# Fifteen tiles of 256 rows and nine of 128 in place of 23 of 256, each operation of three tiles at a step of its own

## The reference

```python
logits = h @ router_weight.T + router_bias
top_vals, top_idx = jax.lax.top_k(logits, 2)
scores = zeros_like(logits).at[arange(T)[:, None], top_idx].set(softmax(top_vals))
gate_up = einsum('th,ehj->etj', h, gate_up_proj) + gate_up_proj_bias[:, None, :]
gate, up = minimum(gate_up[..., ::2], 7), clip(gate_up[..., 1::2], -7, 7)
act = (up + 1) * gate * sigmoid(gate * 1.702)
expert_out = einsum('eti,eih->eth', act, down_proj) + down_proj_bias[:, None, :]
out = x + einsum('te,eth->th', scores, expert_out)
```

## Time and profile before

| | us |
|---|---|
| median of 3 runs | 971.46 |
| lowest, highest | 971.12, 971.56 |
| the profiled execution's own time | 971.87 |
| its span, first to last instruction | 970.1 |
| of it up to the first matmul of an expert | 535.9 |
| of it the expert stage | 434.2 |

### The profile page before, as it was taken

One profiled execution on the slowest core, in us unless ns is written; L12 is line 12 of the kernel. 1 busy time (PEld: TensorE's weight loads), 2 busy tenths in 40 slices (PEclk: granted clock), 3 DMA queues, 4 the chain that ended last, 5 costly groups with the idle time before them and its releaser, 6 DMA issues.

```text
span 970.1 us, 17745 instructions
## 1 busy us (share of the span) xinstructions
PE 865.6 (89%) x7104; PEld 702.1 (72%) x7104; DVE 655.5 (68%) x1356; ACT 464.4 (48%) x735; POOL 314.5 (32%) x348
## 2 busy tenths in 40 slices
PE   5889799897998989889763799999999999999995
PEld 3556567574665756667432799999999999999993
DVE  5654646656466564655564589889888888888872
ACT  4433343333424333333420467677677676676652
POOL 2112221323213232032223233453453454544512
PEclk9999799998999989899675799999999999999998
DMA  8273134171431716126303477687687787786810
GB/s 318 80 251 116 42 131 138 56 253 46 161 104 67 242 57 205 49 73 231 148 11 107 173 239 209 238 242 216 237 234 219 238 235 219 249 220 201 263 55 0
DMA packets 49541, 159.47 MB, mean 164 GB/s; under 512 B 6164, under 2 KB 6420, under 8 KB 40243
## 3 DMA queue, kind: packets, MB, share of 16 engines
q0 software_dynamic: 22368, 98.52, 32.0%
q1 hardware_dynamic: 27090, 59.82, 18.1%
HBM read 103.04 MB, written 58.94 MB: 167 GB/s over the span
## 4 chain that ended last, share of the span: by engine, by line
PE 82%; DVE 6%; ACT 5%; issue 3%; POOL 1%; DMA 1%; SPq 0%; POOLq 0%; another core or an unknown queue 0%; ACTq 0%; DVEq 0%
PE quad L562 9%; PE quad L563 9%; PE quad L564 9%; PE bank L434 7%; PE bank L344 7%; PE bank L337 6%; PE bank L338 6%; PE bank L339 6%; PE bank L370 5%; PE bank L372 4%; PE bank L371 4%; PE quad L395 3%; ACT pt L999 3%; PE quad L415 2%; PE bank L472 2%
## 5 line engine op out<-in xcount | busy, mean ns | idle before, releaser
L562 PE MATMUL quad<-xh,eh 128*128 128x256 f32 x736 | 210.8, 286 | 5.1 <-issue 3.6
L564 PE MATMUL quad<-xh,el 128*128 128x256 f32 x736 | 209.7, 285 | 0.0
L563 PE MATMUL quad<-xl,eh 128*128 128x256 f32 x736 | 209.0, 284 | 0.0
L835 DVE TENSOR_TENSOR el<-raw,eh 128x2048 fp32r<-128x2048 f32 x69 | 158.6, 2299 | 8.8 <-ACT eh L1022 8.8
L562 PEld LDWEIGHTS quad<-xh,eh 128*128 128x128 f32 x736 | 141.0, 192 | 7.5 <-issue 3.8
L563 PEld LDWEIGHTS quad<-xl,eh 128*128 128x128 f32 x736 | 140.6, 191 | 1.8
L564 PEld LDWEIGHTS quad<-xh,el 128*128 128x128 f32 x736 | 139.8, 190 | 0.0
L1022 ACT ACTIVATE eh<-raw 128x2048 fp32r<-128x2048 f32 x69 | 131.6, 1909 | 0.0
L687 DVE TENSOR_REDUCE mx<-quad 128x8 f32<-128x2048 f32 x32 | 73.3, 2292 | 59.7 <-PE quad L395 58.3
L1080 ACT ACTIVATE up<-quad,gb 128x256 f32<-128x256 f32 x92 | 43.6, 474 | 109.8 <-DVE ga L908 109.0
L1196 POOL DMA_INDIRECT out<-ys,ti x46 | 82.1, 1785 | 32.5 <-ACT ys L1094 19.3
(11 more groups left out here) (192 smaller groups left out, 1852.2 us busy)
## 6 DMA issues: line engine op xcount, KB each, us to landing
hs<-wh SPq DMA_DIRECT2D x16, 2084.0 KB, 14.9
xt<-in_x SPq DMA_DIRECT2D x8, 512.0 KB, 5.2
cr<-in_ctxT SPq DMA_DIRECT2D x8, 512.0 KB, 3.9
xb<-in_x SPq DMA_DIRECT2D x8, 512.0 KB, 6.3
out<-xb SPq DMA_DIRECT2D x16, 256.0 KB, 2.0
pt<-in_w SPq DMA_DIRECT2D x3, 1024.0 KB, 6.7
raw<-in_wgb SPq DMA_DIRECT2D x1, 1028.0 KB, 8.1
pt<-in_w SPq DMA_DIRECT2D x4, 256.0 KB, 6.1
```

The costliest lines, as they stand in the source:

```text
L562: e.matmul(o, lh, xh[p][:, c, :], start=c == 0, stop=False)
L563: e.matmul(o, lh, xl[p][:, c, :], start=False, stop=False)
L564: done = e.matmul(o, ll, xh[p][:, c, :], start=False, stop=c == C - 1)
L835: e.tensor_tensor(wl[p][:, part, :], raw[part][:, 0:GW], wh[p][:, part, :].bitcast(F32), ALU.subtract).then_inc(S_(f"e_lo{part}"), 1)
```

## The change

**Two kinds of tile.** `KIND` is S B B seven times, then S B S: 15 large tiles (B, 256 rows) and 9 small ones (S, 128 rows), 24 in all. An expert with u blocks of 128 rows gets large tiles for pairs of blocks and a small one for an odd block; when pairs outnumber the large tiles the rest of them goes to small ones. `tiles()` decides this on DVE by 18 intervals of tiles instead of 8, with arrays of 24 x 18 where it had 23 x 8. One small tile always belongs to expert 0.

**Small tiles.** For these PE holds the rows (128 of them stationary) and moves the weights, 12 matmuls of 512 columns for gate and 12 for up, each half in a bank of its own, plus one matmul of 16 partitions that adds the bias, from a one-hot matrix `oh16` and a table `gbt` that the new `bias_table` makes in the attention stage. The result has rows on partitions. DVE bounds gate and up and multiplies them, ACT takes the sigmoid, each over 128 x 512. Then PE transposes it four times (`turn_act`), and ACT and DVE split it into `ah` and `al`. One `down`, one gather, one add. The three weight parts and their six splits are the same as for a large tile.

**Steps.** `EX` holds a step for each operation of a group of three tiles: S, the B behind it, and the B behind that, called C. The next group's are 92 later. Units, banks, rows and transposes are counted through both kinds.

**The rest.** In `AT` and `ONCE` some steps change; on the engines this moves the transposes of a batch's first k head on PE, and some constants of the first batch on DVE. `bias_table` adds four operations on DVE and two loads of 16 rows.

```diff
-NT = 23
+NT = 24
+BIG = 15
...
+KIND = "SBB" * 7 + "SBS"
...
+BI = before({"B": 1, "S": 0})
+SI = before({"B": 0, "S": 1})
+RI = before({"B": 2, "S": 1})
+UI = before({"B": 4, "S": 2})
...
+SLOT = ["SBC"[i % 3] if KIND[i] == "B" else "S" for i in range(NT)]
...
+GROUP = 92
+EX = {
+    "S": {
+        "turn": -29, "u0": 6, "u1": 8, "act": 35, "down0": 58, "V.xl": -31, "V.gate0": -2, "V.gate1": 18, "V.sl": 32,
...
+def step(i, name):
+    return EX[SLOT[i]][name] + GROUP * (i // 3) + (2 * GROUP // 3 if SLOT[i] == "S" and i % 3 else 0)
+TILES = defaultdict(list)
+for _i in range(NT):
+    for _n in EX[SLOT[_i]]:
+        TILES[step(_i, _n), _n].append(_i)
...
-    "x0": -25, "x1": -19, "k0": -14, "q0": -11, "k1": 4, "q1": 5, "v0": 29, "v1": 35, "hk0": 4, "hq0": 9, "hk1": 24,
+    "x0": -25, "x1": -19, "k0": -14, "q0": -11, "k1": 4, "q1": 5, "v0": 30, "v1": 35, "hk0": -2, "hq0": 9, "hk1": 24,
...
+            def gates_or_ups(i, h):
+                p = i % 2
+                o = bank_of_tile(i, h)
+                for c in range(C):
+                    off = (c % 2) * 1024 + h * 512
+                    rh = wh[p][:, c // 2, off:off + 512]
+                    rl = wl[p][:, c // 2, off:off + 512]
+                    e.matmul(o, xh[p][:, c, 0:128], rh, start=c == 0, stop=False)
+                    e.matmul(o, xh[p][:, c, 0:128], rl, start=False, stop=False)
+                    e.matmul(o, xl[p][:, c, 0:128], rh, start=False, stop=False)
+                P.wait_ge(S_("oh16"), SI[i] + 1)
+                P.wait_ge(S_("gbt"), 1)
+                e.matmul(o, oh16[SI[i] % 2][32:48, :], gbt[:, h * 512:(h + 1) * 512], start=False, stop=True).then_inc(S_("gate_up"), 1)
+            def turn_act(i):
+                P.wait_ge(S_("s_act"), SI[i] + 1)
+                turn(turn_bank(("s", i, 0)), sgs, 4).then_inc(S_("s_turned"), 1)
...
             def down(i, r):
                 p = i % 2
+                n = RI[i] + r
...
-                P.wait_ge(S_("act_lo"), C * i + C)
+                if KIND[i] == "B":
+                    P.wait_ge(S_("act_lo"), C * BI[i] + C)
+                else:
+                    P.wait_ge(S_("s_lo"), SI[i] + 1)
                 P.wait_ge(S_("e_lo2"), i + 1)
...
-            turn_x(0)
-            for i in range(NT + 1):
+                bank_done(P, 6 + n % 2)
+                P.wait_ge(S_("scaled"), n - 1)
+                three(bank[6 + n % 2], lh, ll, rh, rl).then_inc(S_("down"), 1)
+            for s in range(EFIRST, ELAST):
+                for i in tile_at(s, "turn"):
+                    turn_x(i)
+                for i in tile_at(s, "act"):
+                    turn_act(i)
                 for m in range(C):
-                    if i < NT:
-                        gate_up(i, m)
-                    if m == 0 and i + 1 < NT:
-                        turn_x(i + 1)
-                    if m >= 2 and i > 0:
-                        down(i - 1, m - 2)
+                    for i in tile_at(s, f"u{m}"):
+                        if KIND[i] == "B":
+                            gate_up(i, m)
+                        else:
+                            gates_or_ups(i, m)
+                for r in range(2):
+                    for i in tile_at(s, f"down{r}"):
+                        down(i, r)
...
+                P.wait_ge(S_("d_gb"), 32)
+                for h in range(2):
+                    own.done(e.tensor_copy(gbt[:, h * D:(h + 1) * D], gbr[h]))
+                own.wait()
+                for h in range(2):
+                    i = e.scalar_tensor_tensor(out=gbt[:, h * D:(h + 1) * D], in0=gbt[:, h * D:(h + 1) * D].bitcast(F32), scalar=NLG, in1=gbr[h],
+                                               op0=ALU.mult, op1=ALU.add)
...
+                own.done(e.memset(b18[:, :, 0:1], 1.0))
+                own.done(e.tensor_tensor(cn[:], run[:], EBASE, ALU.subtract))
...
+                chain(e.tensor_tensor(cn[:], cn[:], M0, ALU.max))
+                chain(e.tensor_tensor(ci[:], cn[:], CEIL, ALU.add))
+                own.done(e.tensor_scalar(cj[:], ci[:], 7, None, ALU.logical_shift_right))
+                chain(e.tensor_scalar(ck[:], ci[:], 8, None, ALU.logical_shift_right))
+                own.done(e.tensor_copy(uf[:], cj[:]))
+                chain(e.tensor_copy(af[:], ck[:]))
+                own.done(e.tensor_tensor_scan(an[:], onef[:, 0:NE], af[:], 0.0, ALU.mult, ALU.add))
+                chain(e.scalar_tensor_tensor(out=sf[:], in0=af[:], scalar=-2.0, in1=uf[:], op0=ALU.mult, op1=ALU.add))
+                own.done(e.tensor_scalar(ends[:, 1:9], an[:], 2.0, None, ALU.mult))
...
+                own.done(e.tensor_tensor(b18[:, :, 1:NS + 1], PI.unsqueeze(2).to_broadcast([128, NT, NS]),
+                                         ends[:].unsqueeze(1).to_broadcast([128, NT, NS]), ALU.is_ge))
...
+                own.done(e.scalar_tensor_tensor(out=vb[:, 10:18], in0=sf[:], scalar=-128.0, in1=LASTS, op0=ALU.mult, op1=ALU.add))
+                chain(e.tensor_tensor(ohG[:], b18[:, :, 0:NS], b18[:, :, 1:NS + 1], ALU.subtract))
+                for n, v in ((0, vb), (1, vend)):
+                    chain(e.tensor_tensor(pv[:], ohG[:], v[:].unsqueeze(1).to_broadcast([128, NT, NS]), ALU.mult))
                     chain(e.tensor_reduce(bv[:, n, :], pv[:], AX, ALU.add))
...
+                chain(e.tensor_tensor(ohE[:], ohG[:, :, 1:9], ohG[:, :, 10:18], ALU.add))
+                chain(e.tensor_tensor(ohE[:, :, 0], ohE[:, :, 0], ohG[:, :, 0], ALU.add))
+                chain(e.tensor_tensor(pv[:, :, 0:NE], ohE[:], cmt[:, 0:NE].unsqueeze(1).to_broadcast([128, NT, NE]), ALU.mult))
+                chain(e.tensor_reduce(Ei[:], pv[:, :, 0:NE], AX, ALU.add))
+                chain(e.tensor_scalar(gf[:, :, 0], Ei[:], 128.0, PIDX, ALU.mult, ALU.add))
+                e.tensor_copy(wx[:], gf[:, :, 0]).then_inc(S_("wx_set"), 1)
...
+            def gates(i):
+                u = UI[i]
+                P.wait_ge(S_("gate_up"), u + 1)
+                P.wait_ge(S_("s_act"), SI[i])
+                e.tensor_scalar(gus[:, 0, :], bank[u % 4], LIMIT, None, ALU.min).then_inc(S_("gate_in"), 1)
+            def ups(i):
+                u = UI[i] + 1
+                P.wait_ge(S_("gate_up"), u + 1)
+                e.tensor_scalar(gus[:, 1, :], bank[u % 4], LIMIT, -LIMIT, ALU.min, ALU.max).then_inc(S_("gate_in"), 1)
+                P.wait_ge(S_("gate_in"), u + 1)
+                chain(e.scalar_tensor_tensor(out=gus[:, 1, :], in0=gus[:, 1, :], scalar=1.0, in1=gus[:, 0, :], op0=ALU.add, op1=ALU.mult))
+                P.wait_ge(S_("s_sigm"), SI[i] + 1)
+                e.tensor_tensor(sgs[:], gus[:, 1, :], sgs[:], ALU.mult).then_inc(S_("s_act"), 1)
+            def turned_low(i):
+                p = i % 2
+                k = 4 + TURNS.index(("s", i, 0)) % 2
+                P.wait_ge(S_("s_hi"), SI[i] + 1)
+                e.tensor_tensor(al[p][:, :, 0:128], bank[k].rearrange("p (c n) -> p c n", c=4),
+                                ah[p][:, :, 0:128].bitcast(F32), ALU.subtract).then_inc(S_("s_lo"), 1)
...
-            fetch_x(0)
-            fetch_x(1)
-            fetch_w(1, 0)
-            fetch_w(1, 1)
-            for i in range(NT + 1):
-                for m in range(C):
-                    if i < NT:
-                        if m in (2, 3) and i + 2 < NT:
-                            fetch_w(i + 2, m - 2)
-                        if m == 3 and i + 1 < NT:
-                            fetch_w(i + 1, 2)
-                    if m == 0 and i + 2 < NT:
-                        fetch_x(i + 2)
-                    if m == 3 and i > 0:
-                        add_rows(i - 1)
+                        out, bass.IndirectOffsetOnAxis(ap=ti[:, 2 * i + r:2 * i + r + 1], axis=0), ys[n % 2][:], None,
+                        bounds_check=T - 1, oob_is_err=False, compute_op=ALU.add).then_inc(S_(f"d_add{n % 2}"), 16)
+            for s in range(EFIRST, ELAST):
+                for i in tile_at(s, "G.x"):
+                    fetch_x(i)
+                for part in range(3):
+                    for i in tile_at(s, f"G.w{part}"):
+                        if i > 0:
+                            fetch_w(i, part)
+                for i in tile_at(s, "G.add"):
+                    add_rows(i)
...
```

More of the change, by code:

```diff
@@ L37, with before, rows, drained @@
 DW = 2056
+KIND = "SBB" * 7 + "SBS"
+def before(size):
+    return [0] + [int(n) for n in np.cumsum([size[k] for k in KIND])]
+BI = before({"B": 1, "S": 0})
+SI = before({"B": 0, "S": 1})
+RI = before({"B": 2, "S": 1})
+UI = before({"B": 4, "S": 2})
+def rows(i):
+    return range(RI[i + 1] - RI[i])
+def drained(u):
+    i = next(i for i in range(NT) if u <= UI[i + 1])
+    return u, 4 * BI[i] + (u - UI[i] if KIND[i] == "B" else 0)
+SLOT = ["SBC"[i % 3] if KIND[i] == "B" else "S" for i in range(NT)]
@@ new lines, with tile_at @@
+GROUP = 92
+EX = {
[4 rows of a table added]
+    },
[7 rows of a table added]
+    },
[6 rows of a table added]
+        "G.add": 116,
+    },
+}
+def step(i, name):
```

(50 more changed lines are left out.)

304 lines of the change are left out of this document (175 added, 129 removed), and 29 rows, old and new, of tables (AT, EX).

## The result

The changed kernel takes 937.38 us (median of 4 runs, 931.86 to 938.46), the kernel before 971.29 beside it: 0.9647 of before, 95% interval 0.9605 to 0.9688. The forecast was 915, with a range of 905 to 936, so the gain is 34 us where 56 were expected.

What follows compares the result with a forecast made beforehand. PE was taken to bound the expert stage, 17.97 us a tile. Expert stage -49.3, start -6.3 and attention -1 gave -56.6: span 970.1 to 913.5, then +1.8 - 0.4 = 915 us, range 905 to 936.

Steps and rivals of the forecast that it cites:

- PE work of a small tile, of a group: Expert stage on PE: 10.29 us for a small tile, 46.2 for two large tiles and a small one.
- The rule that the prediction takes from the Trainium skill: Weight loads overlap running matmuls only if row groups differ; bias matmuls would cost 0.23, the sum 5 us lower.
- The start: Before the first large tile's matmuls: they start at 548.2 instead of 554.51, -6.3 us, bounds -9 and -2.
- For small waits in seven groups I put 2: Expert stage: 2 us in all for PE's small waits over the seven repeated groups of three tiles.
- the POOL chain: From the second tile's last down to the third tile's gathered rows: 8.7 us, against 8.9 of PE work.
- gather 1.3: Time for POOL to issue the third tile's first gather, within the 8.7 us sum: 1.3 us.
- Each part is issued 4.7 or more ahead of its split: Expert stage: POOL issues each weight part's fetch at least 4.7 us before DVE splits it.
- The walk: One group of three tiles followed in step-table order, each engine in its order, to see who keeps up.
- With 3.4 to spare: DVE load in a group: 42.8 us against PE's 46.2, 93%, with 3.4 to spare.
- Rival A: Each group waits 2 to 5 us, from the level POOL chain or DVE order: 929 to 950 us, 20%.
- Attention, -1 with bounds -3 and +4: Attention stage: moved first k head transposes on PE and four added DVE operations sum to -1 us.
- The tail, 0: From PE's last matmul to the finish: 8.8 us, unchanged.

Runs made afterwards that it cites:

- the control: The kernel before the change, with each of DVE's low weight splits written as two halves: 970.10 us, 0.9993 of before.

## Why the prediction was wrong

- **PE work of a small tile, of a group: right** (10.0 for 10.29; 46.2 for 46.2). Two small slips cancel in a large tile: by rows 4 a unit takes 2.92 and not 2.88, and the distances leave 0.69 for the eight transposes and not 0.87. The rule that the prediction takes from the Trainium skill ("TensorE: Matmul & The Clock Gate", section "The mechanism") does not fit the new trace either: the bias matmul, of another row group, costs 0.52 and not 0.23, and the loads of 128 rows cost nothing extra.
- **The start: right in this profile, less in others.** -5.9 for -6.3. `tiles()` takes 8.05 us (7.8) and now sets the first gather, since the scatters have landed. But in the other eight traces of changed kernels the stretch takes 37.4 to 40.3 us and not 37.3, -5.8 to -2.9: PE waits 2.9 to 5.5 us for tile 1's rows. That is inside the bounds of -9 and -2, and what comes late is what was named with them, the rows.
- **"For small waits in seven groups I put 2": the step that failed.** It stood on the POOL chain, 8.7 us against a cover of 8.9, called level. Its term "gather 1.3" came from a row of the kernel before, in which that issue meets no split. In the new order it met one in 5 of 7 groups and took 3.2. PE stood 11.2 us for it, then 7.9 more for DVE, and lost 3.7 to low clock. The prediction costed DVE and POOL each alone.
- **"Each part is issued 4.7 or more ahead of its split": wrong.** The walk had POOL free when a buffer was. DVE waited for `eh` 25.4 us in 8 places, up to 5.2 us. "With 3.4 to spare" on DVE was then used up by those gaps; its load itself (42.4 a group for 42.8) was right.
- **Rival A was what happened**: its signs (`xs` at the third tile, `el` at the small tile's first unit, low clock behind) are the two largest rows of waits, its price of 2 to 5 us a group was 4.3, its time of 929 to 950 held. Its cause was only half named: the level chain on POOL was, but not that a split on DVE holds an issue on POOL. At 20% it was too cheap, since the sum itself called its chain level.
- **Attention, -1 with bounds -3 and +4: wrong by 9.5** (7.5 to 9.5 by the medians of the two exchanged tables). I priced the moved transposes by their own 0.4, and not by the waits of 0.6 and up to 1.7 that PE's list of waits showed beside them. Without this the time would have been 946 (the run with the old table), 31 over the forecast: that the total missed by only 22 is luck, two misses of opposite sign.
- **The tail, 0: +2.3.** The small last tile's add waits 4.09 us for the add before it to land; before, the last adds were two of one tile.

```profile
918.10 1.55 POOL L1450 DMA_INDIRECT out<-ys,ti  x1 [1.04 <-ACT ys L1343]
923.75 1.56 POOL L1450 DMA_INDIRECT out<-ys,ti  x1 [4.09 <-DMA out<-ys,ti]
```

Open: why runs of one kernel differ by up to 7 us, where those of the kernel before mostly lie within 3 or 4. The expert stage of the run with the old attention table has the order of the changed kernel, and there PE waited 28.8 us in place of 21.6; so the time at which POOL's issues meet the splits may be what varies. The start varies too, by the 3 us told above. No run tested either.

## What to carry to other kernels

Before a DMA issue on POOL is priced, look what DVE runs at that moment: a long operation with two inputs from SBUF adds what is left of itself. Put gathers and weight fetches whose buffers are free ahead of adds that wait, and write DVE's long two-input operations in two pieces where POOL issues beside them; either gave 9 to 12 us here, both 20. A chain that comes out level in the sum is a wait: give it the price of its rival.

## What the runs showed of the hardware

- An issue on POOL that begins inside a DVE split (2048 columns, two SBUF inputs, 2.28 us) ends 0.81 to 0.89 us after it (23 of 23 in the expert stage; the 8 adds 1.44 to 1.49); one that begins 0.01 to 0.02 us after the split's start is not held (20 of 20, 0.94 us), one that begins 0.08 after it is (20 of 20 in the control, 1.96 to 1.97 us with a piece of 1024 columns).
- A scatter issued on POOL inside a DVE reduction of 2.29 us with one input, in PSUM, is not held (8 of 8, 0.96 us).
- Two splits of 1024 columns take 2.36 us for 2.29, four of 512 take 2.5.
- A matmul of 16 partitions between two of 128 starts 0.33 us behind the one ahead, the next 0.42 behind it and the one after that 0.34, where the others are 0.23 apart.
